# Causal attention: later keys zeroed after the exponential, and the row maxima of the last query tile taken through a rectified difference of two key halves

## The reference

```python
B, T, D = x.shape                      # 4, 1024, 128
H = decay_logits.shape[0]              # 16 heads of dh = 8
qkv = (x @ qkv_w.T + qkv_b).reshape(B, T, 3, H, dh)
q, k, v = ...
scores = jnp.einsum('bhtd,bhsd->bhts', q, k) * scale
causal = jnp.triu(jnp.ones((T, T), dtype=bool), 1)
scores = jnp.where(causal, -jnp.inf, scores)
attn = jax.nn.softmax(scores, axis=-1)
seq_out = jnp.einsum('bhts,bhsd->bhtd', attn, v)
```

## Time and profile before

| | value |
|---|---|
| runs, median (lowest to highest) | 1975.96 us (1975.79 to 1977.72) |
| profiled execution | span 1971.5 us; its own device time is not given apart from the span |
| PE, DVE, ACT, POOL busy in the span | 1906.8, 1623.9, 1483.3, 916.0 us |
| mean granted clock of TensorE | 0.986 of 2.4 GHz |
| prologue and phase 2, from the first maximum to the last exponential's values | 728.9 to 1161.0 us |

### The profile page before, as it was taken

How to read it: one execution, slowest core, us unless ns; L and a number is a source line. 1 busy time by engine, 2 the same in 40 slices (tenths; PEclk the granted TensorE clock), 3 DMA queues, 4 the chain that set the end, 5 groups by cost and what they waited for, 6 DMA issues and landing times. The chain is left out here.

```text
span 1971.5 us, 52907 instructions
## 1 busy us (share of the span) xinstructions
PE 1906.8 (97%) x18490; PEld 1129.9 (57%) x18490; DVE 1623.9 (82%) x5453; ACT 1483.3 (75%) x4089; POOL 916.0 (46%) x549
## 2 busy tenths in 40 slices
PE   7999999999999989999999999899999999999998
PEld 4777763577775343434434367437777646777743
DVE  6999964899994579999999769779999548999844
ACT  5999993799997253777777754469999837999962
POOL 2787860578781040000000046337878406787700
PEclk9999999999999997999999999999999999999999
DMA  6121220112120040111111000002212201121301
GB/s 188 43 48 43 48 60 6 35 43 49 42 66 23 6 152 28 41 42 42 42 42 43 19 5 2 2 21 47 49 43 47 55 6 42 42 49 42 70 12 43
DMA packets 76106, 85.08 MB, mean 43 GB/s; under 512 B 17139, under 2 KB 50499, under 8 KB 75715
## 3 DMA queue, kind: packets, MB, share of 16 engines
q1 hardware_dynamic: 75647, 81.68, 16.3%
q10 hardware_dynamic: 196, 0.02, 0.0%
HBM read 21.14 MB, written 8.39 MB: 15 GB/s over the span
## 5 line engine op out<-in xcount | busy, mean ns | idle before, releaser
L304 ACT ACTIVATE probs<-probs,negmax 128x128 f32<-128x128 f32 x1024 | 399.8, 396 | 23.2 <-DVE negmax L377 22.1
L2083 ACT ACTIVATE gprobs<-ps_global 128x1024 f32<-128x1024 f32 (+3 forms) x384 | 291.4, 810 | 124.3 <-PE ps_global L1548 101.2
L259 POOL TENSOR_TENSOR rot<-rot 128x1024 f32<-128x1024 f32 x128 | 302.5, 2363 | 145.6 <-DVE rot L347 145.6
L265 POOL TENSOR_TENSOR qk<-rot,cnorm 128x1024 f32<-128x1024 f32 x128 | 243.8, 1905 | 120.1 <-POOL rot L259 89.5
L272 POOL TENSOR_TENSOR probs<-probs,iden 128x1024 f32<-128x1024 f32 x128 | 242.9, 1898 | 120.0 <-DVE iden L385 120.0
L1778 DVE TENSOR_REDUCE maxes<-ps_global 128x1 f32<-128x512 f32 (+2 forms) x384 | 222.0, 637 | 10.2 <-PE ps_global L1511 6.5
L377 DVE CUSTOM_DVE_ANT_0 probs<-ps_attn,masks 128x128 f32<-128x128 f32 x1024 | 226.2, 285 | 0.0
L1506 PE MATMUL ps_global<-kq 48*128 48x512 bf16 (+3 forms) x768 | 196.7, 345 | 7.2 <-DVE maxes L1778 1.8
L304 ACT ACTIVATION_READ_ACCUMULATOR probs<-probs,negmax 128x1 f32 x1024 | 197.0, 192 | 0.0
L345 DVE TENSOR_TENSOR rot<-ps_attn,rotary 128x512 f32<-128x512 f32 x256 | 174.8, 683 | 1.8 <-PE ps_attn L171 1.6
L239 PEld LDWEIGHTS ps_attn<-probsT,v_first 128*64 128x64 f32 x2048 | 118.1, 136 | 98.1 <-ACT probsT L325 94.3
(11 more groups left out here) (212 smaller groups left out, 4585.0 us busy)
## 6 DMA issues: line engine op xcount, KB each, us to landing
v_first<-v_second SPq DMA_DIRECT2D x256, 128.0 KB, 2.3
hs<-z_a SPq DMA_DIRECT2D x256, 32.0 KB, 1.9
ln<-z_b SPq DMA_DIRECT2D x56, 128.0 KB, 2.4
kq<-split_scratch SPq DMA_DIRECT2D x64, 96.0 KB
kq<-split_scratch SPq DMA_DIRECT2D x64, 64.0 KB
split_scratch<-parts SPq DMA_DIRECT2D x8, 384.0 KB, 4.1
split_scratch<-gprobs SPq DMA_DIRECT2D x6, 384.0 KB, 3.9
x_tok<-in_x_dram SPq DMA_DIRECT2D x4, 512.0 KB, 6.4
```

Source lines behind the costliest of these rows:

```text
L259: nc.gpsimd.tensor_tensor(a, a, b, ALU.add).then_inc(C["rot_sum"], 1)
L265: nc.gpsimd.tensor_tensor(qk[:, k % 2, :].rearrange("p (h d) -> p h d", d=DH), rot_a[:, k % 2, :, :], cnorm[:, k % 2, :].unsqueeze(2).to_b ...
L304: last = nc.scalar.activation(probs[:, k % 2, slot, :], probs[:, k % 2, slot, :], ACT.Exp, scale=-1.0, bias=negmax[:, k % 2, slot:slot + 1 ...
L2083: nc.scalar.activation(probs[:, step % RING, 2 * p:2 * p + 2, 0:w], ps[:, S0 + 2 * p:S0 + 2 * p + 2, 0:w], ACT.Exp).then_inc(C["p2_exp"], 1)
```

## The change

Four things change in the global attention.

First, the scores of phase 2 get no mask products. After the exponential GpSimd's `hide_later` sets the entries of later keys in the diagonal block (128 keys x 4 heads x 128 queries) to zero, and `values` of such a unit waits for that (`p2_hidden`) instead of the exponential. TensorE's `values` is moved back by one unit: unit `u` issues `values` of unit `u - 1`. `copy_out` moves back by one unit too.

Second, for the last tile of each slot (tiles 4 to 7 in slot 0; 4, 5 and 7 in slot 1) the maxima are taken in another way. With a the scores of the first half of the keys and b those of the second, max(a, b) = a + max(b - a, 0). A fill of kind `GAP` writes b - a: the product with the second half's keys, a second product of the negated queries with the first half's keys, and two mask products. ScalarE rectifies it into SBUF (`keep_gap`, Relu) and frees the bank. A fill of kind `SUM` later writes a, and VectorE adds what was kept and reduces, in one instruction. The negated queries are made by GpSimd (`negate`). Tile 7 has 8 fills as before. `in_turn` lays the four `GAP` fills among the fills of tile 6. `FILLS_AT` stays as it is.

Third, slots 0 and 1 have 44 fills each; before the first unit 71 fills and turns are issued (`USES_BEFORE`). Each bank has its own semaphore, since two engines free banks.

Fourth, GpSimd's order: negations, the split of the maxima and `hide_later` follow each other by hand, and in slot 15 the last four `hide_later` stand behind `body(-2)`, `outer_products(0)` and `subtract(1, 0)`, `subtract(1, 1)`.

```diff
+PLAIN, GAP, SUM = range(3)
...
+def p1_folded(t, kind):
+    half = (t + 1) * TILE // 2
+    return [(t, half if kind == GAP else 0, half, r, (p,), kind) for p in range(2) for r in range(2)]
+def in_turn(one, other):
+    other = [other[k ^ 1] for k in range(len(other))]
+    pairs = [pair if k % 2 == 0 else pair[::-1] for k, pair in enumerate(zip(one, other))]
+    return [fill for pair in pairs for fill in pair] + one[len(other):]
+def slot_fills(n):
+    short = p1_fills(0) + p1_fills(1)
+    if n >= 2:
+        return (short + sum((p1_fills(t) for t in range(2, 6)), []) + in_turn(p1_fills(6), p1_folded(7, GAP)) + p1_folded(7, SUM))
+    begun = short + in_turn(p1_fills(2), p1_folded(4, GAP)) + in_turn(p1_fills(3), p1_folded(5, GAP))
+    if n == 1:
+        return begun + p1_folded(4, SUM) + p1_folded(5, SUM) + in_turn(p1_fills(6), p1_folded(7, GAP)) + p1_folded(7, SUM)
+    return (begun + in_turn(p1_folded(4, SUM), p1_folded(6, GAP)) + in_turn(p1_folded(5, SUM), p1_folded(7, GAP)) +
+            p1_folded(6, SUM) + p1_folded(7, SUM))
+FILLS = [slot_fills(n) for n in range(SLOTS)]
 TURN_AFTER = 2
...
+NEGATED = [(0, 4), (0, 5), (0, 6), (0, 7), (1, 4), (1, 5), (1, 7)] + [(n, 7) for n in range(2, SLOTS)]
+NEGATED_AT = {use: (k if k < 6 else k % 2) for k, use in enumerate(NEGATED)}
...
+USES_BEFORE = USES - (SLOTS - 1) * sum(sum(counts) for counts in FILLS_AT) + AHEAD - 1
...
+        shelf = sb("parts", [P, 2 * GROUP * CHUNK])
+        early = shelf[:, 0:2 * PARTS * CHUNK]
...
+        def released(use):
+            return C[f"p1_free{use % RING}"]
+        def await_release(eng, use):
+            eng.wait_ge(released(use), C.after(f"p1_free{use % RING}", use // RING + 1))
+        def kept(n, t, r, p):
+            at = (GROUP * ((n if n >= 2 else t) % 2) + 2 * p + r) * CHUNK
+            return shelf[:, at:at + CHUNK]
...
+                if kind == GAP:
+                    pe.wait_ge(C["p1_negated"], C.after("p1_negated", NEGATED.index((n, t)) + 1))
                 rows, half = half_rows(r, SPLIT_ROWS), half_rows(r, 64)
-                masked_here = on_diagonal(P1_FILLS[f]) and len(both) == 2
+                masked_here = on_diagonal(FILLS[n][f]) and (len(both) == 2 or kind == GAP)
...
                 for a, p in enumerate(both):
                     out = ps[:, bank_of(use), a * w:(a + 1) * w]
-                    mm = nc.tensor.matmul(out, qs[buf][rows, p, tile_cols(t)], ks[buf][rows, p, CHUNK * c:CHUNK * c + w],
+                    mm = nc.tensor.matmul(out, qs[buf][rows, p, tile_cols(t)], ks[buf][rows, p, first:first + w],
                                           start=True, stop=not masked_here, skip_group_check=True)
+                    if kind == GAP:
+                        nc.tensor.matmul(out, negated[rows, NEGATED_AT[n, t], p, :], ks[buf][rows, p, 0:w],
+                                         start=False, stop=False, skip_group_check=True)
...
-                diagonal = t0 == s * TILE
                 for r in range(2):
                     rows = half_rows(r, FULL_ROWS)
                     mm = nc.tensor.matmul(ps[:, S0 + 2 * p + r, 0:w], ks[buf][rows, p, tile_cols(s)], qs[buf][rows, p, t0:t0 + w],
-                                          start=True, stop=not diagonal, skip_group_check=True)
-                if diagonal:
-                    for r in range(2):
-                        half = half_rows(r, 64)
-                        nc.tensor.matmul(ps[:, S0 + 2 * p + r, 0:64], A["causal"][half, FIRST, :],
-                                         A["causal"][half, CAUSAL_K, 64:128], start=False, stop=False, skip_group_check=True)
-                    for r in range(2):
-                        half = half_rows(r, 64)
-                        mm = nc.tensor.matmul(ps[:, S0 + 2 * p + r, 0:TILE], A["causal"][half, SECOND, :],
-                                              A["causal"][half, CAUSAL_K, :], start=False, stop=True, skip_group_check=True)
+                                          start=True, stop=True, skip_group_check=True)
...
-                pe.wait_ge(C["p2_exp"], C.after("p2_exp", 2 * step + 2))
+                if t0 == s * TILE:
+                    pe.wait_ge(C["p2_hidden"], C.after("p2_hidden", DIAGONALS * n + diagonals_to(u)))
+                else:
+                    pe.wait_ge(C["p2_exp"], C.after("p2_exp", 2 * step + 2))
...
-            for use in range(FILLS + AHEAD):
+            for use in range(USES_BEFORE):
...
-                    values(n, u)
+                    if (n, u) != (0, 0):
+                        values(*divmod(U2 * n + u - 1, U2))
...
+            values(SLOTS - 1, U2 - 1)
...
+                if kind == SUM:
+                    await_release(dve, partner(n, f))
+                    nc.vector.tensor_tensor_reduce(bank, bank, kept(n, t, r, p0)[:, 0:w], 1.0, LEAST, ALU.add, ALU.max,
+                                                   maxes[:, n % 2, r, p0, t, c:c + 1]).then_inc(released(use), 1)
+                elif on_diagonal(FILLS[n][f]) and len(both) == 1:
+                    nc.vector.tensor_tensor_reduce(bank, bank, later[:, CHUNK - w:CHUNK], 1.0, LEAST, ALU.add, ALU.max,
+                                                   maxes[:, n % 2, r, p0, t, c:c + 1]).then_inc(released(use), 1)
+                else:
+                    nc.vector.reduce_max(maxes[:, n % 2, r, p0:p1, t, c], bank.rearrange("q (p s) -> q p s", s=w), AX_X
+                                         ).then_inc(released(use), 1)
...
+            def hide_later(n, u):
+                c, s, t0 = P2_UNITS[u]
+                if t0 == s * TILE:
+                    gp.wait_ge(C["p2_exp"], C.after("p2_exp", 2 * (U2 * n + u) + 2))
+                    block = probs[:, (U2 * n + u) % RING, :, 0:TILE]
+                    nc.gpsimd.affine_select(block, block, [[0, GROUP], [1, TILE]], ALU.is_ge, 0.0, base=0, channel_multiplier=-1
+                                            ).then_inc(C["p2_hidden"], 1)
+            def negate(n, t):
+                gp.wait_ge(C[f"qk_in{n % RING}"], C.after(f"qk_in{n % RING}", 16 * QK_DMAS * (n // RING + 1)))
+                k = NEGATED.index((n, t))
+                at = NEGATED_AT[n, t]
+                for m, g in NEGATED[0:k]:
+                    if NEGATED_AT[m, g] == at:
+                        last = max(p1_use(m, f) for f, fill in enumerate(FILLS[m]) if fill[0] == g and fill[-1] == GAP)
+                        gp.wait_ge(C["p1_filled"], C.after("p1_filled", last + 1))
+                nc.gpsimd.tensor_scalar(negated[:, at, :, :], qs[n % RING][:, :, tile_cols(t)], -1.0, None, ALU.mult
+                                        ).then_inc(C["p1_negated"], 1)
+            for n, t in NEGATED[0:6]:
+                negate(n, t)
+            split_max(0)
+            for n, t in NEGATED[6:7]:
+                negate(n, t)
+            for n in range(SLOTS):
+                for u in range(4):
+                    hide_later(n, u)
+                if n + 1 == SLOTS:
+                    break
+                split_max(n + 1)
+                if n + 2 < SLOTS:
+                    negate(n + 2, S_TILES - 1)
+                for u in range(4, U2):
+                    hide_later(n, u)
...
+            body(-2)
+            outer_products(0)
+            subtract(1, 0)
+            subtract(1, 1)
+            for u in range(4, U2):
+                hide_later(SLOTS - 1, u)
+            normalise(1, 0)
+            normalise(1, 1)
+            for t in range(S_TILES + 2):
...
+                    if step >= 1:
+                        for part in ((0,), (1, 2))[p]:
+                            keep_gaps(uses_after(*before, part))
...
+            def keep_gap(n, f):
+                t, first, w, r, both, kind = FILLS[n][f]
+                use = p1_use(n, f)
+                act.wait_ge(C["p1_filled"], C.after("p1_filled", use + 1))
+                for m, g in KEPT_BEFORE.get((n, t), ()):
+                    await_release(act, p1_use(m, FILLS[m].index((g, 0, (g + 1) * TILE // 2, r, both, SUM))))
+                nc.scalar.activation(kept(n, t, r, both[0])[:, 0:w], ps[:, bank_of(use), 0:w], ACT.Relu
+                                     ).then_inc(released(use), 1)
...
-            for m in range(CHUNKS - DEEP, CHUNKS):
+            for m in (DEEP, DEEP + 1):
+                act.wait_ge(C[f"pj_written{m % DEEP}"], C.after(f"pj_written{m % DEEP}", written_count(m)))
+            keep_gaps(range(USES_BEFORE))
+            for m in (DEEP - 2, DEEP - 1, DEEP + 2):
                 act.wait_ge(C[f"pj_written{m % DEEP}"], C.after(f"pj_written{m % DEEP}", written_count(m)))
             for n in range(SLOTS):
                 for u in range(U2):
                     exp(n, u)
-                    if u == 0 and n >= 1:
+                    if u == 1 and n >= 1:
                         copy_out(n - 1, 1)
-                    if u == 4:
+                    if u == 5:
```

(29 more changed lines are left out.)

82 lines of the change are left out of this document (39 added, 43 removed).

## The result

| | before | after |
|---|---|---|
| median of 4 runs (lowest to highest) | 1976.7 (1975.8 to 1977.7) | 2011.4 (2010.3 to 2012.1) |
| ratio, 95% interval | | 1.0176 (1.0162 to 1.0191) |
| profiled span | 1971.5 | 2010.1 |

A forecast was written before the change was run, and what follows sets the result against it. VectorE's maxima were taken to set the pace of 15 slots and the prologue. Slots +17.4, prologue -6 and slot 15 +1.5 gave +13 us: span 1984.5, median 1989 us, range 1957 to 2008.

The forecast's parts named there:

- The steady slot: Steady slots: VectorE idles while TensorE works through gap fills; period +1.2 us a slot, +17.4 us in all (3 to 26).
- The prologue: Before the first unit: VectorE's 34 us fall to 24, but 28 us taken for the prologue; -6 us (-11 to +4).
- That gap fills can't overlap: Units 1 and 2 of a steady slot: two GAP fills run in turn, 1.01 us a pair, +0.79 and +0.83.
- I take the clock as rising part of the way in: Prologue: a TensorE that never rests gets a granted clock above 0.7, before 0.54; 28 us, so -6 us.
- The -8: Prologue term by the skill's rule that sustained activity releases the throttled clock: -8 us instead of -6.
- Slot 15: Last slot: masks give -1.6, selects behind the second subtraction delay values and normalising, +3; together +1.5 us (0 to +4).
- From the span to the median: Whole kernel: the median of the runs lies 4.5 us above the profiled span, so 1984.5 becomes 1989 us.
- The select: GpSimd, diagonal units: 1.3 us for 512 elements, between 0.66 and 2.00; hidden in the steady part up to 2.0 us each.
- the rectification: ScalarE, four of 512 a slot: 0.5 us each, 2.0 us a slot on 19 us of work, below 24.
- Rival C: GpSimd's selects cost 3 us and values waits each time: 26.5 us of GpSimd work a slot, +32, 2008 us; chance 0.08.
- A: Whole kernel: VectorE stays the bound everywhere and all of its 46 us is gained, 1930 us; chance 0.10.
- B: Slots: gap fills overlap or idle time is made good later; period +0.15, 1970 us in all; chance 0.18.

The follow-up runs named there:

- The fold alone: Kernel before with only the last tiles' maxima taken through GAP and SUM fills; values not moved, no selects: 2016.6 us with mask products, 2011.1 us without.
- the light runs: VectorE's maxima read 32 columns instead of up to 512: kernel before 1951.6 us, with selects and later values only 1948.1, changed kernel 1982.4.

## Why the forecast was right in direction and wrong in size

- **The steady slot: mechanism right, size too small.** VectorE's waits of about 2 and 1.4 us were 1.82 and 1.50, its start on unit 3 6.34 for 6.6, its share 83% as forecast, and the slot read lasts 25.8. That 6.34 is so near 6.6 is partly luck. That gap fills can't overlap was wrong, 1.0 us too much for the two pairs; against it stood 0.2 that the masks didn't give back and the wait of 0.46 for ScalarE, which was missing. The term was +1.2, measured +1.54 (with 15 periods +23.1 for +17.4). What was too small is the rest of the slot: from unit 3 to the end of unit 11 I had the length of before less 0.25 (18.65), and it is 984.97 - 965.51 = 19.46, with VectorE waiting there for TensorE again and again. The fold alone does the same, so the later values are not its cause. Why a saving can turn into a loss shows best in the light runs: a floor stood 1.0 us below the old period, and I never worked it out, though the earlier trace rows had TensorE busy 49.45 of 50.
- **The prologue: the step that failed.** This is the only term that left its own range (-11 to +4): -6 was forecast and +8.6 measured at the first `neg_max`; from the first maximum to the first exponential, where the prologue ends, it is +9.1. It failed at "I take the clock as rising part of the way in". The windows of after:

```profile
741.00:746.00 5.00, 4.79 (x28) 2.17 (x24) 2.98 (x10) 1.85 (x4) 0.00 (x0) 0.50 0.17 64
746.00:751.00 5.00, 2.39 (x14) 1.00 (x14) 1.67 (x6) 1.96 (x4) 1.67 (x2) 0.50 0.08 30
...
766.00:771.00 5.00, 4.87 (x30) 2.06 (x27) 3.10 (x11) 2.54 (x6) 0.56 (x1) 0.50 0.05 12
```

  The clock stays at 0.50 (1.2 GHz), also where TensorE is busy 4.8 or 4.9 of 5 us. The kernel before had shown the same, and I read only its mean of 0.54:

```profile
741.00:746.00 5.00, 4.75 (x12) 0.90 (x10) 5.00 (x13) 0.00 (x0) 0.00 (x0) 0.50 0.13 52
746.00:751.00 5.00, 4.81 (x15) 1.26 (x15) 5.00 (x15) 0.00 (x0) 0.00 (x0) 0.50 0.00 0
...
766.00:771.00 5.00, 5.00 (x63) 2.31 (x61) 3.23 (x6) 2.74 (x5) 0.00 (x0) 0.73 0.16 62
```

  In both kernels it rises only after phase 2 has begun beside the fills, with the first exponentials at 764.20 and 776.11 (before, then after). In the kernel after, it is still 0.50 from 776 to 781 and 0.88 from 781 to 786:

```profile
764.20 1.94 ACT L2083 ACTIVATE gprobs<-ps_global 128x1024 f32<-128x1024 f32 x2 [35.91 <-PE ps_global L1548]
```
```profile
776.11 3.83 ACT L2194 ACTIVATE gprobs<-ps_global 128x1024 f32<-128x1024 f32 x5 [2.99 <-PE ps_global L1604]
```

  No run has a prologue at 2.4 GHz, so what the clock alone is worth there stays open. The step's other premise, a TensorE that never rests there, was wrong too: it is busy 23.0 of 35 us. I had no term for its wait on the first negation (3.98 us of idle, 1.6 on the path) and none for the reuse of the kept halves (3.5), both to be read from the order of GpSimd's and ScalarE's code; 3.7 us stay open. The count of columns before was also low: by the code it is 33,500 and not 31,200. The -8 worked out by the Trainium skill's page "TensorE: Matmul & The Clock Gate", section on the HAM clock gate, falls with it: the trace doesn't agree, since in the kernel before TensorE was busy 4.2 to 4.9 of every 5 us from 736 to 766 us and the clock stayed at 0.50.
- **Slot 15: right place, small.** `values` waited 1.91 behind the second subtraction as forecast; +2.7 in the slot for +1.5, and 1.5 to 3.1 over the kernels with the same tail.
- **From the span to the median.** The 4.5 us added for what lies around the span was too much. In every run on record that has both, the time lies 1.7 to 2.0 us above its own span. So the profiled execution of before took about 1973.3 us, less than the three runs beside it.
- **The select** was taken as 1.3 us and is 0.64, just under the lower bound of 0.66; the rectification as 0.5, and two of 512 take 1.08. Rival C is out: from 800 to 1100 us GpSimd ends no wait of TensorE, and `values` waits for a select in slot 15 alone, 1.91 and 0.95 us.
- **Rivals A and B.** VectorE's saving did come, and it bought nothing, so A is refuted. The Trainium skill's rule in "Perfetto Trace Analysis", section "Identifying the Most-Contended Engine", is to optimize the engine with the highest occupancy first. It did not pay here: VectorE's share fell from 97% to 83%, the relief put work on engines that had hardly any time to spare, and the kernel got slower. B's condition came true (the gap fills overlap) and its time did not.

## What to carry to other kernels

Before moving work off the busiest engine, find the floor of the others: a version in which that engine's operations are made nearly empty is one run, and here it would have shown that at most 1.0 us a slot can be won, while the new work raises the floor by 1.46. Take a change of several parts one by one and in both orders: the later values cost 1.0 us a slot without the fold, and with it the selects and later values together cost nothing. Where three engines pass a few banks in order, an engine's share may fall by 14 points and its idle time is no one's gain. And read the first stage, with its lower clock, as a kernel of its own: more than half of the forecast's error was there.

## What was not expected of the hardware

- GpSimd's affine select of 128x512 in float32 takes 0.64 us, as fast as its cast of 512, and VectorE's reductions keep their length beside it (682 ns before, 683 after for 512 columns, 790 to 1110 us).
- Two accumulating chains of products in opposite row halves, each in its own bank, run side by side, product by product: 0.52 us a pair at 2.4 GHz.
- In the kernel before, the granted clock stayed at 0.50 from 736 to 766 us, with TensorE busy 4.2 to 4.9 of every 5 us.
